# Loading the weight addresses of all expert tiles into VectorE's registers at once

## The reference, cut to what matters

```python
# _L1_ffn_ref: one expert of eight per token
scores = feats @ centroids.T
expert = jnp.argmax(scores, axis=1)
ys = layernorm by the expert's gamma and beta, then relu(h @ W1e.T + b1e) @ W2e.T + b2e
...
# _L3_ffn_ref: two experts of eight per token, and a shared expert for all
topk_w, topk_i = jax.lax.top_k(softmax(xt @ gate_w.T), 2)
a = jax.nn.silu(g) * u            # g, u: products with gate_k, up_k (128 x 512 per expert)
eo = a @ down_k                   # 512 x 128 per expert
shared = jax.nn.silu(xt @ sh_gate) * (xt @ sh_up) @ sh_down
```

## Time and profile before

| | |
|---|---|
| median of 3 runs | 729.12 us (727.24 to 729.53) |
| profiled execution | 721.61 us, its span 719.8 us |
| PE matmul busy | 636.2 us (88%) |
| DVE busy | 465.0 us (65%) |
| ACT busy | 329.9 us (46%) |
| POOL busy | 214.6 us (30%) |
| mean granted TensorE clock | 0.968 |

### The profile page before, as it was taken

The page is one execution under the profiler, slowest core; times in us unless marked ns, Lnnn a source line. Parts: engine busy times, 40 slices in busy tenths (PEclk is TensorE's granted clock), DMA queues, the critical chain, the costliest instruction groups (busy, mean ns, idle before and its releaser), DMA issues.

```text
span 719.8 us, 13302 instructions
## 1 busy us (share of the span) xinstructions
PE 636.2 (88%) x5242; PEld 481.0 (67%) x5242; DVE 465.0 (65%) x953; ACT 329.9 (46%) x552; POOL 214.6 (30%) x190
## 2 busy tenths in 40 slices
PE   5999888998999998978869998789999989769992
PEld 4655556676667675877757555666676767669992
DVE  6688777678676565733545888776765557515562
ACT  4368652225665654115612777556656431113330
POOL 4000011002445536252330000114556351624441
PEclk9999999999999999998989999999999999989996
DMA  8600000024020320012066000000203200140003
GB/s 340 280 2 1 1 1 1 0 80 186 1 61 3 88 55 6 1 39 73 30 236 294 1 2 1 1 1 2 61 2 89 61 1 1 46 115 26 25 26 98
DMA packets 11852, 42.09 MB, mean 58 GB/s; under 512 B 1808, under 2 KB 7024, under 8 KB 10320
## 3 DMA queue, kind: packets, MB, share of 16 engines
q1 hardware_dynamic: 9808, 36.99, 15.1%
q0 software_dynamic: 1984, 4.26, 1.8%
HBM read 36.36 MB, written 7.68 MB: 61 GB/s over the span
## 4 chain that ended last, share of the span: by engine, by line
PE 64%; DVE 15%; POOL 7%; issue 7%; ACT 4%; DMA 3%; DVEq 1%; SPq 0%; POOLq 0%; ACTq 0%
PE banks L1911 6%; PE banks L946 6%; PE banks L934 5%; PE banks L195 4%; PE banks L453 4%; PE banks L511 4%; PE banks L197 3%; PE banks L196 3%; POOL sorted_rows L1634 3%; PE banks L983 3%; PE banks L1922 3%; DVE work L738 2%; PE banks L1426 2%; PE banks L962 2%; POOL work L1127 2%
## 5 line engine op out<-in xcount | busy, mean ns | idle before, releaser
L1127 POOL TENSOR_TENSOR work<-work 128x512 f32<-128x512 f32 x64 | 86.0, 1354 | 115.9 <-ACT work L1091 115.7
L738 DVE TENSOR_REDUCE work<-banks 128x2 f32<-128x512 f32 x128 | 84.5, 688 | 24.8 <-PE banks L453 18.4
L284 POOL TENSOR_TENSOR ln_rstd<-ln_var_eps,minus_half_and_newton 128x4 f32<-128x4 f32 x16 | 17.2, 1074 | 176.5 <-DVE ln_var_eps L250 167.8
L946 PE MATMUL banks<-work 128*64 128x256 f32 x512 | 64.1, 388 | 4.0 <-ACT work L1091 3.5
L934 PEld LDWEIGHTS banks<-work_split 64*128 64x128 f32 x768 | 47.7, 186 | 12.6 <-issue 8.0
L946 PEld LDWEIGHTS banks<-work 128*64 128x64 f32 x512 | 32.8, 136 | 32.5 <-ACT work L1091 16.4
L934 PE MATMUL banks<-work_split 64*128 64x256 f32 x768 | 54.2, 287 | 0.2
L1185 DVE TENSOR_TENSOR work_split<-banks,work_split 128x512 fp32r<-128x512 f32 x32 | 22.0, 686 | 43.5 <-ACT work_split L1071 43.4
L1091 ACT ACTIVATE work<-work,small_operands 128x1024 f32<-128x1024 f32 x32 | 36.8, 1150 | 28.6 <-DVE work L1197 28.1
L1197 DVE SCALAR_TENSOR_TENSOR work<-banks,score_floor,raw_b 128x1024 f32<-128x1024 f32 x32 | 39.6, 1278 | 11.6 <-PE banks L934 11.6
L1911 PE MATMUL banks<-work 128*128 128x128 f32 x368 | 46.4, 281 | 0.2 <-ACT work L1951 0.2
(11 more groups left out here) (319 smaller groups left out, 1492.9 us busy)
## 6 DMA issues: line engine op xcount, KB each, us to landing
raw_b<-in_wf SPq DMA_DIRECT2D x1, 6528.0 KB, 24.9
raw_a<-in_wf SPq DMA_DIRECT2D x1, 4632.0 KB, 14.1
raw_b<-reciprocal_rows SPq DMA_DIRECT2D x6, 512.0 KB, 5.6
raw_a<-reciprocal_rows SPq DMA_DIRECT2D x6, 512.0 KB, 5.4
raw_a<-in_wf SPq DMA_DIRECT2D x1, 2048.0 KB, 13.3
raw_b<-in_wb SPq DMA_DIRECT2D x1, 2048.0 KB, 17.5
raw_a<-in_wb SPq DMA_DIRECT2D x1, 2048.0 KB, 9.9
sorted_rows<-in_blank SPq DMA_DIRECT2D x1, 1656.0 KB, 24.4
```

What stands on the lines that cost most here:

```text
L738: nc.vector.tensor_reduce(a_nm[:, t:t + 2, j], bank(7 - n % 2).rearrange("p (e k) -> p e k", e=2), AX.X, ALU.max, negate=True).then_inc(A[ ...
L946: last = nc.tensor.matmul(ps[DH * h:DH * (h + 1), 4, (b % 2) * S:(b % 2 + 1) * S], w_v[:, 2 * b + kb, (2 * p + h) * DH:(2 * p + h + 1) * D ...
L1127: nc.gpsimd.tensor_tensor(w_ps[g % 2].rearrange("p (h q) -> p h q", h=2), v[:, :, 0, :], v[:, :, 1, :], ALU.add).then_inc(W["ps"].sem, 1)
```

## The change

`tiles_dve` now ends with one call that loads all tiles' addresses into VectorE's registers, with the same range for each as before, and returns the values. `weights(j)` of both stages uses value j instead of loading it. The diff, whole:

```diff
@@ tiles_dve
             order.step(nc.vector.tensor_scalar(tile_at[:, 0:n], tile_e[:, 0:n], float(E - 1), float(width), ALU.min, ALU.mult))
+            return nc.values_load_multi_w_load_instructions(tile_at[0:1, 0:n], engines=[mybir.EngineType.DVE],
+                                                            min_val=0, max_val=(E - 1) * width)[1]
@@ f1_dve
-            tiles_dve(order, 0, W_F1)
+            at = tiles_dve(order, 0, W_F1)
@@ f1_dve, weights(j)
-                at = dve.value_load(tile_at[0:1, j:j + 1], min_val=0, max_val=(E - 1) * W_F1)
-                nc.vector.tensor_copy(g_w[j % 3], raw_a[:, bass.ds(at, W_F1)]).then_inc(G["w"], 1)
+                nc.vector.tensor_copy(g_w[j % 3], raw_a[:, bass.ds(at[j], W_F1)]).then_inc(G["w"], 1)
@@ f3_dve
-            tiles_dve(order, 1, W_F3)
+            at = tiles_dve(order, 1, W_F3)
@@ f3_dve, weights(j)
-                at = dve.value_load(tile_at[0:1, j:j + 1], min_val=0, max_val=(E - 1) * W_F3)
-                nc.vector.tensor_copy(k_w[j % 3], raw_b[:, bass.ds(at, W_F3)]).then_inc(K["w"], 1)
+                nc.vector.tensor_copy(k_w[j % 3], raw_b[:, bass.ds(at[j], W_F3)]).then_inc(K["w"], 1)
```

## The result

The changed kernel takes **724.71 us** (median of 4 runs, 722.74 to 724.78) against 728.98 us before (727.24 to 729.53): ratio 0.9939, 95% interval 0.9915 to 0.9963. That is 4.4 us less, with 2.7 to 6.2 as bounds. It is faster by more than 0.3%; 724.3 was predicted.

A forecast was written before the change was run, and what follows sets the result against it. First-stage tiles were taken as bound by a chain through VectorE, second-stage tiles by TensorE. First stage -4.9 us and second stage's front +0.1 us gave -4.8, 724.3 us against the median, range 720.4 to 729.2.

The forecast's parts named there:

- Out of the first stage's tiles: First stage's copies: load and check leave the chain (-3.7 us), copies shorten by 0.20 us each (1.2); -4.9 us.
- The floor: First stage's turn of two tiles: 4.08 us after the change, VectorE's chain still setting the pace, TensorE just behind.
- Into the front of the first stage: Ahead of the first stage's tiles: one load and 15 checks, 4.8 us, covered by the sorted rows' DMA; nothing.
- Into the front of the second stage: Ahead of the second stage's tiles: 7.0 us of slide, 1.8 uncovered, 1.7 back by the higher clock; net +0.1 us.
- I take one load at 0.556: Front of either stage: a bulk load priced as the trace's dearest load of one value, 0.556 us.
- Out of the second stage's tiles: Second stage's tiles: 23 loads and checks, all beside a full TensorE; nothing gained.
- The sum: Whole kernel: -4.9 + 0.1 = -4.8 us, against the median 724.3 us.
- Register by register: Both fronts: bulk load fetches values one after the other, 0.30 us each; second stage +6.4, 730.6 us; chance 0.12.
- Warm start: Second stage: checks cheaper in a row, slide just under 5.2 us, tiles on time at full clock; -6.6, 722.5 us; chance 0.18.
- POOL first: First stage: POOL's instruction beats the copy, which waits for its end, 0.20 us later per turn; 730.4 us; chance 0.06.
- Slower: Second stage's front: 23 loads of 0.556 us plus checks, 19.2 us of slide; +7.4, 736.5 us; chance 0.09.
- the values are fetched again at each use: Both stages' copies: no register kept per tile, so no effect; 729.1 us; chance 0.03.

The follow-up runs named there:

- e11: Kernel before, with the range check taken out of the first stage's copies and the load left in; 26.75 us from first to thirteenth result.
- e3: Kernel before, with only the second stage's addresses loaded at once; slower than the kernel before by 0.55% (0.28 to 0.82), 4.0 us.
- e9: The changed kernel once more, no edit; ratio 0.9951 to the kernel before, 3.6 us less.
- e1: The kernel before once more, no edit; profiled span 726.0 us, stages at their old lengths.
- e2: Kernel before, with only the first stage's addresses loaded at once, the second's at each copy; ratio 0.9928.
- e5: Changed kernel without the range check of each value in both bulk loads; second stage 98.96 us.
- e10: First-stage addresses at once, second's at each copy, unread matmuls 77 instead of 60 (first stage) and 62 instead of 40 (second); 717.97 us, ratio 0.9858.
- e4: Changed kernel with the second stage's bulk load behind VectorE's four products of the shared expert; ratio 0.9942.
- e6: Changed kernel with the second stage's 23 values loaded by 23 loads, each with its check, at the same place; 729.68 us, ratio 1.0017.
- e7: Changed kernel with 20 instead of 40 unread matmuls ahead of the second stage's tiles; second stage 98.81 us.
- e8: First-stage addresses at once, second's at each copy, 62 instead of 40 unread matmuls ahead of the second stage's tiles; second stage 99.47 us.

## Why the prediction was right, and where it was not, point by point

- **Out of the first stage's tiles** (-4.9 predicted): right. 29.70 to 24.76 us, 4.94. Its two terms are apart in e11: the check and the shorter copy give 29.75 - 26.75 = 3.0 us, the load of 0.30 us the other 2.0 (six times 0.33). That the copy would be 0.20 us shorter was right; the reason given, that it comes ahead of POOL, holds for the change but isn't the condition (e11). POOL's home DMA pays more than forecast, 1.52 us and not near 1.24, at no cost to the stage.
- **The floor**: right. The turn from 344.67 to 348.75 takes the 4.08 us that were worked out; over all six the mean is 4.13, as the second of them is longer (338.42 to 342.77, 4.35; before it was 335.35 to 340.53, 5.18). The chain through VectorE still sets the pace, with TensorE just behind it, though the view of the waits names TensorE alone: the links are those of the earlier trace rows, and e11 shows each 0.33 us off VectorE given back in full.
- **Into the front of the first stage** (nothing): right. From the address row to the first result 21.32 us, before 21.35, though the first copies begin at 319.71, 6.7 us behind the addresses.
- **Into the front of the second stage** (+0.1): the one term that was wrong. It measured +2.7 in the two first profiles; over all profiles, the change, e3 and e9 have 103.4 to 103.9 us, before, e1, e2 and e11 101.2 to 101.7, means 103.6 and 101.5, so +2.1. The mechanism was right, and so were the checks (23 x 0.28 = 6.4; 6.3 by e5) and the 1.7 us of clock that come back (1.74). By the prediction's own last sentence this term failed: it was to be wrong if the tiles began more than 4 us later against the sorted rows' arrival. They begin 4.45 us later, counted from the addresses; counted from the landing of the first rows (637.32 + 2.4 = 639.7 by the DMA's issue and its time to landing) it is still some 4.1. Two sizes were off. The step "I take one load at 0.556" is the first: 2.15 us for 23 values. The second wasn't in the sum: TensorE's shared units took 6.50 us instead of 5.29, 1.2 more; that the longer idle ahead of them is the reason is not shown, since e10 has 6.11 behind the old idle of 4.13. The slide of the unread matmuls was 28.55 - 18.75 = 9.8 us, not 7.0, and 4.45 of it uncovered, not 1.8.
- **Out of the second stage's tiles** (nothing): right. e2 loads each address at its copy, e4 all of them ahead of the tiles where nobody waits, and the stage takes 101.74 and 101.41 us.
- **The sum.** By the stages of all profiles the change is worth -4.9 + 2.1 = -2.8 us, by the runs -4.4 (first) and -3.6 (e9), each within 2 us either way. The predicted -4.8 lies inside the first interval, and partly by luck: by the stages it is 2 us too much, all of it the second stage's front, and an error of that size is as large as what the medians leave open.
- **The rivals.** Register by register is e6: 730.6 was worked out for it, 729.68 measured; the real load was nearer to one load than to 23. The Trainium skill's page "Runtime: NRT & Kernel Launch" (Instruction fetch mechanics) gives some 200 ns per register even for a bulk load, of registers loaded from HBM. Here, from SBUF, it was 2.15 us for 23, 0.093 each, and the measurement decides. Its direction, that a bulk load isn't one load's price, was right. Warm start was not reached by the change, and its reason did not hold (a check in a row costs 6.3 / 23 = 0.27 us, against 0.28); it was reached by e5 and e7, where it measured what the rival had given it or a little more (the stage at 98.96 and 98.81, 2.3 and 2.4 us under 101.22). POOL first did not arise in the change, where the copy comes first; e11, where POOL does, shows that the copy isn't held (0.77 us). Slower needed 14.0 us of slide; it was 9.8. That the values are fetched again at each use is ruled out by the view of line L1626, which has all loads of the addresses in two. Of the Trainium skill's page "SBUF — State Buffer" (Who interferes with whom) the rule that the first to issue holds the port pair and the other fully blocks nearly fits the change, where POOL's instruction grows by 0.57 us behind a copy that began 0.08 earlier (held to the copy's end, it would have grown by 0.69); it doesn't fit e11, where POOL began 0.25 earlier and was still the one that grew.

## What to carry to other kernels

A register load with its range check is sequencer work that the busy share doesn't count; where an engine's wait, load and instruction form one chain, it is paid in full (0.62 us of a turn of 4.95 here). Taking it out of a loop into the front was free only where nobody waited at the front: the same eight microseconds cost nothing behind the products (e4) and some 2 us ahead of them. And where the values are known to be in range, the check can go: without it the bulk load was hidden even ahead of the products (e5).

## What the runs showed of the hardware that was not expected

- A load of several registers: 1.81 us for 15 values, 2.15 for 23, 0.30 for one. Between the two larger ones a value costs 0.043 us; most of the price is there at 15 already.
- TensorE's slow spell behind an idle stretch isn't ordered by the length of the idle. The shared units' eight matmul records behind 4.14 us of idle took 5.29 us, behind 12.74 us 6.50 (the change), behind 6.42 us 6.63 (e5), behind 18.50 us 5.20 (e6); and behind the same 4.13 us they took 5.40 (e8) and 6.11 (e10). In the change the granted clock was 0.50 and 0.62 in the two stretches ahead of 631.3 us, and 1.00 from there:

```profile
625.00:628.80 3.80, 3.78 (x5) 1.72 (x6) 0.56 (x1) 0.00 (x0) 2.88 (x3) 0.50 0.16 58
628.80:631.30 2.50, 2.50 (x5) 1.00 (x4) 0.69 (x1) 0.60 (x1) 1.91 (x2) 0.62 0.19 59
631.30:634.90 3.60, 3.60 (x33) 3.55 (x32) 2.68 (x5) 0.60 (x1) 2.82 (x3) 1.00 0.11 41
```

  After 1.44 us of idle (e5) the clock stayed at 1.00. What sets the spell's length was not tried.
- POOL's indirect DMA and VectorE's copy hinder each other by when they meet: with the copy 0.08 us ahead POOL takes 1.52 us, with POOL 0.25 ahead 1.14, and with POOL 0.55 ahead POOL keeps its 0.95 and the copy takes 0.97 instead of 0.77.
